# Pair attention with 15 steps a tile: |a| folded into the projections, and VectorE adding the two feature halves of one row block in eight

## What is computed

```
mask = where(adj > 0, 0, -1e22)
q = feat @ W1.T                      # 2048 x 64
k = feat @ W2.T                      # 2048 x 64
e = relu(q[None, :, :] + k[:, None, :])      # for each pair (i, j): 64 features
scores[i, j] = sum_d e[i, j, d] * a[d]
out = softmax(scores + mask) @ feat
```

## Time and profile before

| | |
|---|---|
| median of three runs | 12600.37 us (12598.65 to 12601.54) |
| profiled execution, span | 12601.2 us |
| TensorE busy | 12319.6 us (98%) |
| VectorE busy | 9716.6 us (77%) |
| ScalarE busy | 9590.5 us (76%) |
| mean granted TensorE clock | 0.993 |
| matmuls of the pair stage (L1254) | 7128.4 us busy |

### The profile page before, as it was taken

How to read it: one execution, slowest core, us unless ns; L and a number is a source line. 1 busy time by engine, 2 the same in 40 slices (tenths; PEclk the granted TensorE clock), 3 DMA queues, 4 the chain that set the end, 5 groups by cost and what they waited for, 6 DMA issues and landing times.

```text
span 12601.2 us, 250115 instructions
## 1 busy us (share of the span) xinstructions
PE 12319.6 (98%) x109953; PEld 6079.0 (48%) x109953; DVE 9716.6 (77%) x13670; ACT 9590.5 (76%) x8545; POOL 419.2 (3%) x636
## 2 busy tenths in 40 slices
PE   7999999999999999999999999999999999999999
PEld 3333853338533384333843338433384334843348
DVE  4888848888488885888758887588875888758887
ACT  3888748887488874888749887488874888758886
POOL 1000000000000000000000000000000000000000
PEclk9999999999999999999999999999999999999999
DMA  2000320003200031000310003100031000310003
GB/s 76 20 19 18 103 81 21 18 18 110 78 18 18 18 117 70 18 18 18 126 61 18 18 22 129 54 18 18 23 137 46 18 18 27 139 40 18 21 24 107
DMA packets 205754, 610.39 MB, mean 48 GB/s; under 512 B 45057, under 2 KB 136833, under 8 KB 139137
## 3 DMA queue, kind: packets, MB, share of 16 engines
q1 hardware_dynamic: 183792, 450.72, 10.4%
q0 software_dynamic: 20880, 143.66, 3.1%
HBM read 556.47 MB, written 8.39 MB: 45 GB/s over the span
## 4 chain that ended last, share of the span: by engine, by line
PE 91%; DVE 7%; ACT 1%; issue 1%; SPq 0%; DMA 0%; POOL 0%; DVEq 0%
PE ps L1254 53%; PE ps L1236 10%; PE ps L1338 7%; PE ps L1351 4%; PE ps L1411 4%; PE ps L1267 4%; PE ps L1318 4%; PE ps L1176 2%; PE ps L1397 2%; DVE E L799 1%; DVE E L800 1%; DVE PT L826 1%; PE ps L1219 1%; DVE T L922 1%; DVE E L801 1%
## 5 line engine op out<-in xcount | busy, mean ns | idle before, releaser
L1254 PE MATMUL ps<-E,a_win 128*32 128x512 f32 x65536 | 7128.4, 594 | 31.0 <-ACT E L566 19.6
L1254 PEld LDWEIGHTS ps<-E,a_win 128*32 128x32 f32 x65536 | 2136.4, 110 | 4827.8 <-issue 4683.3
L566 ACT ACTIVATE E<-Q,ka 128x2048 f32<-128x2048 f32 x2048 | 4075.4, 1990 | 0.0
L799 DVE TENSOR_SCALAR E<-Q,kd 128x2048 f32<-128x2048 f32 x2048 | 2630.4, 1284 | 982.4 <-PE ps L1254 957.5
L565 ACT ACTIVATE E<-Q,ka 128x1280 f32<-128x1280 f32 x2048 | 2786.2, 1360 | 783.6 <-PE ps L1254 759.6
L800 DVE TENSOR_SCALAR E<-Q,kd 128x2048 f32<-128x2048 f32 x2048 | 2625.5, 1282 | 0.0
L801 DVE TENSOR_SCALAR E<-Q,kd 128x768 f32<-128x768 f32 x2048 | 1265.6, 618 | 0.0
L922 DVE CUSTOM_DVE_ANT_0 T<-ps,adj_ring 128x2048 f32<-128x2048 f32 x512 | 1172.1, 2289 | 88.7 <-PE ps L1318 85.9
L599 ACT ACTIVATE T<-T,nmin 128x2048 f32<-128x2048 f32 x512 | 1028.1, 2008 | 217.2 <-DVE nmin L922 217.1
L1338 PE MATMUL ps<-ident,T 128*128 128x128 f32 x8192 | 1098.5, 276 | 17.1 <-DVE HT L884 12.3
L1338 PEld LDWEIGHTS ps<-ident,T 128*128 128x128 f32 x8192 | 913.1, 141 | 198.7 <-ACT PT L471 71.0
(11 more groups left out here) (131 smaller groups left out, 7578.1 us busy)
## 6 DMA issues: line engine op xcount, KB each, us to landing
adj_ring<-in_adj SPq DMA_DIRECT2D x384, 1024.0 KB, 5.1
adj_res<-in_adj POOLq DMA_DIRECT2D x128, 1024.0 KB, 6.5
qcur<-AGG SPq DMA_DIRECT2D x896, 16.0 KB, 2.8
qcur<-HT SPq DMA_DIRECT2D x896, 16.0 KB, 2.2
HW<-in_x POOLq DMA_DIRECT2D x9, 1024.0 KB, 7.2
X<-in_x SPq DMA_DIRECT2D x128, 64.0 KB, 1.9
out_x<-X SPq DMA_DIRECT2D x8, 1024.0 KB, 17.0
wq_r<-in_L_gnn_Wq SPq DMA_DIRECT2D x4, 64.0 KB, 2.6
```

The lines of the kernel that those rows point to most:

```text
L566: nc.scalar.activation(E[:, s + 3, :], Q2[:, :], ACT.Relu, bias=ka[:, u, 48 + m:49 + m]).then_inc(e_act, 1)
L799: nc.vector.tensor_scalar(E[:, s, :], Q2[:, :], kd[:, u, m:m + 1], 0.0, ALU.add, ALU.max)
L1254: last = mm(ps[QROWS * grp:QROWS * (grp + 1), 4 * u + c, :], win, E[:, s + grp, c * CH:(c + 1) * CH], start=(m == 0), stop=(m == QUADS - 1 ...
```

## The change

**One row is now half the features of four rows i.** Partitions hold 32 features of four rows. A tile's 32 row blocks (8 in each of the four column groups) have a first half (features 0 to 31) and a second half (32 to 63), 64 rows of E as before. `QA` and `QB` hold the queries of either half four times over, `KLO`, `KHI`, `KBN` and `KBP` the keys of all tiles, made once a batch.

**|a| is folded into the projections.** Since |a| relu(q + k) is relu(|a|q + |a|k), the weights are scaled by |a| with signs when the program starts, and `s_win` holds only signs. Keys are held negated (all but `KBP`), and relu(q + k) is written as max(q, -k) (they differ by k, which is the same for all j and drops out of the softmax). A first half is given the sign of its second half's a: where the signs agree it is max(QA, KLO), else min(QA, KHI), so its operation is a maximum and a minimum with two per-partition scalars, one of which has no effect. ScalarE still makes a relu, with `KBP` as bias.

**One block in eight is added up before TensorE.** With like signs in both halves, VectorE can add them: in one block of each column group it makes the first half and then, with one scalar_tensor_tensor, adds max(QB, KBN) to it in place. That block takes one row of E, not two. A column group has 7 x 2 + 1 = 15 rows, a tile 15 steps of 4 (`NS`). `PLAN` says for each step and column group which half or sum it is and whether ScalarE makes it: 26 second halves a tile go to ScalarE, all whole rows; VectorE makes 28 first halves alone, 4 sums and 2 second halves. Every slot of E now comes round after three steps.

**Around it.** Each chunk of queries takes two matmuls, the keys 8 of 256 columns a half; VectorE copies the QB chunks and makes the key tables from PSUM, ScalarE copies QA. Keys of the first half go ahead of the last chunk's queries. `PT1` is now a name for HW, so that x is fetched behind the stage. The tail's places move with the shorter tile: minimum after step 1, exp after 3, transposes after 5, both copies after 7, product after 9, `finish1` after 11. Eight small loads and 15 more small VectorE operations stand at the program's start.

The diff, cut to its core:

```diff
 EQ = 3
-SPLIT = 768
-TURN = QUADS + QUADS // 2
+FUSED = (4, 8, 6, 12)
+NS = 2 * SETS - 1
+SCALAR_TWO = tuple(k for k in range(NS) if k != 1)
+def column_group(g):
+    kinds, m = [], 0
+    while len(kinds) < NS:
+        if len(kinds) == FUSED[g]:
+            kinds.append(("fused", m))
+        else:
+            kinds += [("first", m), ("second", m)] if g < 2 else [("second", m), ("first", m)]
+        m += 1
+    return kinds
+def tile_plan():
+    plan = []
+    for row in zip(*[column_group(g) for g in range(4)]):
+        left = 2 if len(plan) in SCALAR_TWO else 1
+        step = []
+        for kind, m in row:
+            by_act = kind == "second" and left > 0
+            left -= by_act
+            step.append((kind, m, by_act))
+        plan.append(step)
+    return plan
...
+        PT1 = HW
...
             for k in range(LN_EARLY, LN_MID):
                 rstd_step(b, k)
+            pool.wait_ge(x2_rdy, (b + 1) * NT)
+            fetch(b + 1 if more else b)
             fetched_rstd(b + 1)
...
-            def quad(T, m, u, first):
-                nc.scalar.activation(E[:, s + 2, SPLIT:N], Q2[:, SPLIT:N], ACT.Relu, bias=ka[:, u, 32 + m:33 + m])
-                nc.scalar.activation(E[:, s + 3, :], Q2[:, :], ACT.Relu, bias=ka[:, u, 48 + m:49 + m]).then_inc(e_act, 1)
+            def step1(b, t, k):
+                n = t * NS + k
+                if n >= EQ:
+                    act.wait_ge(e_used, b * NT * NS + n - EQ + 1)
+                for g, (kind, m, by_act) in enumerate(PLAN[k]):
+                    if by_act:
+                        col = k_col(t, g, m)
+                        last = nc.scalar.activation(E[:, e_slot(t, k) + g, :], QB[:, :], ACT.Relu, bias=KBP[:, col:col + 1])
+                last.then_inc(e_act, 1)
...
+            def evac_k1(b, half):
+                dve.wait_ge(qk1_ps, b * 10 + (7, 10)[half])
+                nc.vector.tensor_scalar(KBP[:, cols], of_b, -1.0, None, ALU.mult)
+                nc.vector.tensor_copy(KBN[:, cols], of_b)
+                nc.vector.tensor_scalar(KLO[:, cols], of_a, same[:, :], low_off[:, :], ALU.mult, ALU.add)
+                nc.vector.tensor_scalar(KHI[:, cols], of_a, other[:, :], high_off[:, :], ALU.mult, ALU.add).then_inc(k1_sb, 1)
...
+                add = None
+                for g, (kind, m, by_act) in sorted(enumerate(PLAN[k]), key=lambda x: x[1][0] != "fused"):
+                    if by_act:
+                        continue
+                    if kind == "second":
+                        last = nc.vector.tensor_scalar(dst, QB[:, :], KBN[:, col:col + 1], None, ALU.max)
+                    else:
+                        last = nc.vector.tensor_scalar(dst, QA[:, :], KLO[:, col:col + 1], KHI[:, col:col + 1], ALU.max, ALU.min)
+                    if kind == "fused":
+                        last.then_inc(e_first, 1)
+                        add = dst, col
+                if add:
+                    dve.wait_ge(e_first, (b * NT + t) * 4 + at + 1)
+                    last = nc.vector.scalar_tensor_tensor(out=dst, in0=QB[:, :], scalar=KBN[:, col:col + 1], in1=dst,
+                                                          op0=ALU.max, op1=ALU.add)
+                last.then_inc(e_dve, 1)
...
+                evac_qb(b, 0)
                 normalise(b, LN_1, chunk_of(NC - 1), X, H, zn_rdy)
+                evac_qb(b, 1)
+                evac_qb(b, 2)
+                evac_k1(b, 0)
+                evac_qb(b, 3)
...
+            def keys1(b, half):
+                pe.wait_ge(qa_sb, b * NC + half + 1)
+                rows = HT[:, :].rearrange("p (n r) -> p n r", r=GR)
+                for at, w in ((0, wka), (256, wkb)):
+                    for r in range(GR):
+                        last = mm(ps[GP * r:GP * (r + 1), 4 + half, at:at + 256], w[:, :],
+                                  rows[:, half * 256:(half + 1) * 256, r], start=True, stop=True,
+                                  tile_position=(0, GP * r))
+            def queries1(b, c):
+                for bank, w in ((4 + c, wqa), (c, wqb)):
+                    mm(ps[:, bank, :], w[:, :], HT[:, c * CH:(c + 1) * CH], start=True, stop=True).then_inc(qk1_ps, 1)
...
                 for c in range(NC):
-                    for grp in range(4):
-                        last = mm(ps[QROWS * grp:QROWS * (grp + 1), 4 * u + c, :], win,
-                                  E[:, s + grp, c * CH:(c + 1) * CH], start=(m == 0), stop=(m == QUADS - 1),
-                                  tile_position=(0, QROWS * grp))
+                    for g, (kind, m, by_act) in enumerate(PLAN[k]):
+                        win = s_win[:, QROWS - GR - GR * m:2 * QROWS - GR - GR * m]
+                        last = mm(ps[QROWS * g:QROWS * (g + 1), 4 * u + c, :], win,
+                                  E[:, s + g, c * CH:(c + 1) * CH], start=(k == 0), stop=(k == NS - 1),
+                                  tile_position=(0, QROWS * g))
```

## The result

The changed kernel takes 12303.23 us (median of 4 runs, 12302.36 to 12303.74), the kernel before, run beside it, 12600.96 (4 runs, 12598.65 to 12601.7). The ratio is 0.9764, with a 95% interval of 0.9751 to 0.9778: 2.4% faster. The forecast was 12364 us, 61 us too much; that lies within its own range, 13 us above its lower end.

The account below looks back on a forecast made before the run. TensorE was taken to bound the pair stage before, VectorE to set the tile after. 8 x (-33.1 + 2.7) + 6.5 = -236.7 us on 12601.2 gave 12364 us; own range 12,290 to 12,440.

Parts of the forecast that it names:

- The two-pointer first half: VectorE's first half with KLO and KHI at 128x2048: 1.35 us long, 1.265 start to start, a pointer costing 0.063.
- case 1: Pair stage: TensorE still sets the tile if the second pointer costs nothing; some 57.6 us a tile, 12,175 us; chance 0.10.
- VectorE's sum 57.6 and a wait of 1.2: Pair-stage tile: VectorE's work of 57.6 us plus a 1.2 us wait at `finish1` for the value product, 58.8 us.
- The layer-norm tiles: Three of the 15 intervals between tiles hold four layer-norm operations, charged 1.0 us each; average 59.08 us after.
- The average before, 61.17: Pair stage before the change: mean of tiles of 60.87 and 61.47 us, from which the 59.08 after was subtracted.
- the forecast's first tile: First tile of the pair stage, without tail: 60.2 us before, 58.5 after, paced by VectorE, 1.7 less.
- The seam, +2.7 us a batch: Before the pair stage: keys ahead of the last query product +1.0, two query matmuls +1.9, VectorE's earlier copy -0.2.
- The start, +6.5 us: Program start, once: eight more small loads 4.4 us, fifteen tiny VectorE operations and five waits 2.1; range 4 to 10.
- The fetch of x at no cost: Next x's fetch moves on POOL behind the stage: 45 us of cover, no cost; uncovered, up to 10 us a batch.
- Case 2: Pair stage: VectorE sets the tile with more waits than found; at 1 us more a tile, 12,492 us; chance 0.17.
- Case 3: VectorE's first halves: the second pointer takes the double pace away, 2.33 us start to start, 16,730 us; chance 0.07.
- case 4: Pair stage: the tile doesn't shorten, VectorE's waits adding up to TensorE's old pace; about 12,600 us; chance 0.04.

## Why the prediction was right, and where its sizes were off

The mechanism held: the step that goes shortens TensorE's tile, VectorE takes over as the bound, and the tile ends where VectorE's sum and its one wait put it. TensorE's standstill is smaller than forecast, 0.8 us a tile and not 1.4, and stands at one of the four fused steps alone. The last transposes ahead of the stage stand at 250.22 and 11218.79 us in the first and the last batch before, at 251.47 and 10956.41 after: a batch takes 1566.9 us before and 1529.3 after, 37.6 less, where the sum had 33.1 - 2.7 = 30.4. That is 58 us over eight, and the start gives the other 5. The terms one by one:

**The two-pointer first half, 1.265 start to start.** It is 1.257 [the row of 436.60]. The duration of 1.339 stands against 1.35. Over 32 operations that is 0.3 us a tile. The experiment with one pointer gives the second pointer 0.060 us; the rows before gave 0.063 and 0.054, and the price was the right one to argue on, as it decided between this case and case 1. The Trainium skill's table, "VectorE: DVE Perf Modes", section "The perf-mode tier table (the rule you actually need)", has 1227 ns for this shape without a charge for pointers; no form with a pointer agrees with it here (1279 for one, 1339 for two).

**VectorE's sum 57.6 and a wait of 1.2: 58.8 us a tile.** The wait is 1.28, the tile 58.40, so the sum is 57.1: 0.5 less, of which the first halves are 0.3. This is one mis-sized term. The layer-norm tiles go the other way: the forecast gave each of the three 1.0 us more than a plain tile, and it is 1.7 (60.09 against 58.40), with the slot wait of 0.49 among it.

**The average before, 61.17.** I took the mean of two plain tiles. The rows behind them show that three of 14 intervals were longer before as well. TensorE's timeline before, and after:

```profile
338.62 1.97 PE L1176 MATMUL ps<-ident,T 128*128 128x128 f32 x16
...
583.29 1.97 PE L1176 MATMUL ps<-ident,T 128*128 128x128 f32 x16
...
613.86 0.66 PE L1304 MATMUL ps<-ident,AGG 128*128 128x128 f32 x4
...
645.49 1.97 PE L1176 MATMUL ps<-ident,T 128*128 128x128 f32 x16
...
1197.16 1.97 PE L1176 MATMUL ps<-ident,T 128*128 128x128 f32 x16
```

```profile
337.10 1.97 PE L1270 MATMUL ps<-ident,T 128*128 128x128 f32 x16
...
1160.24 1.97 PE L1270 MATMUL ps<-ident,T 128*128 128x128 f32 x16
```

From 583.29 to 645.49 it is 62.20 us: TensorE makes four transposes of normalised features there (L1304), on top of the longer tile's work. I charged the layer-norm work to the tiles after and not to those before. Over the 14 intervals of batch 0, from 338.62 to 1197.16 before and from 337.10 to 1160.24 after, the mean is 61.32 before (forecast 61.17) and 58.80 after (forecast 59.08): 2.53 a tile and not 2.09. The 0.44 are the largest mistake: 6.2 us a batch, 49 in all, a third of it the average before and two thirds the tile after.

**The rest of the stage.** The stage is 980.1 - 941.2 = 38.9 us shorter, and 33.1 were forecast. The 14 intervals give 35.4; its two ends give 3.5, where the forecast's first tile and one more interval make 1.7 + 2.1 = 3.8.

**The seam, +2.7 us a batch (bounds 1 and 5).** In batch 0 the first write of E came 4.3 us behind the start of the last transposes (250.22, key copy at 254.31 and 0.2 long); it comes 5.3 behind them after. That is +1.0, at the lower bound. (Sixteen key matmuls follow the last transposes there, and not eight; the eight of the second half are done at 257.88, while VectorE writes the first rows, and TensorE then waits 2.9 us for its first step.) TensorE and VectorE there, after:

```profile
251.47 0.66 PE L1277 MATMUL ps<-ident,H 128*128 128x128 f32 x4 [1.05 <-ACT H L528]
252.06 1.09 PE L1286 MATMUL ps<-HT,wka 128*32 128x256 f32 x8
...
253.98 1.13 PE L1294 MATMUL ps<-HT,wqa 128*128 128x512 f32 x2
254.94 1.02 PE L1294 MATMUL ps<-HT,wqb 128*128 128x512 f32 x2
```

```profile
256.79 2.60 DVE L881 TENSOR_SCALAR E<-QA,KLO,KHI 128x2048 f32<-128x2048 f32 x2
```

The term that was mis-sized is the 2.08 us that I carried over for the last query product: it takes 1.13, its partner 1.02. The windows show the clock: for before the stretches ahead of batch 1's transposes and from there to the first step, for after the same, and the first 3 us of the stage (columns as in the earlier trace rows):

```profile
1813.03:1818.03 5.00, 1.59 (x3) 0.30 (x3) 2.71 (x13) 1.25 (x3) 2.99 (x4) 0.61 0.00 2
1818.03:1826.26 8.23, 5.10 (x11) 1.54 (x11) 3.65 (x5) 5.28 (x7) 1.30 (x1) 0.50 0.00 0
```

```profile
1776.08:1781.08 5.00, 1.98 (x4) 0.68 (x5) 4.00 (x16) 1.25 (x3) 2.99 (x4) 1.00 0.00 0
1781.08:1790.38 9.30, 6.43 (x41) 2.04 (x41) 6.81 (x10) 5.67 (x6) 1.30 (x1) 1.00 0.00 0
1790.38:1793.38 3.00, 3.00 (x16) 0.95 (x20) 3.00 (x3) 3.00 (x2) 0.00 (x0) 0.51 0.02 5
```

Before, the clock is at its lower level (0.50, 1.2 GHz) throughout this seam of batch 1; after, it is at 1.00 (2.4 GHz) there and falls to the lower level at the stage's first step, where TensorE has waited 2.9 us and VectorE sets the pace anyway. In four batches, the first among them, a low stretch lies ahead of the transposes too (0.66 in the 5 us before 251.47). In batch 1 the seam is only +0.55: the first write of E stands 4.77 behind the transposes before (1822.80) and 5.32 after (1786.40). Taking 0.6 a batch, the term was 2.1 too large, 17 us over eight. The prediction had named the doubt ("that may have changed by then"), but took the slow value; the seams of the other batches would not have settled it, as the query pair takes 2.08 us in all of them before.

**The start, +6.5 us.** SP's queue and POOL, which answer to the earlier trace rows:

```profile
6.38 3.90 SPq L372 DMA_DIRECT2D a<-in_L_gnn_a  x8
```

```profile
36.72 8.44 POOL L498 DMA_DIRECT2D adj_res<-in_adj  x16
```

The eight loads take 3.90 us (4.4 were said), and the adjacency is issued at 36.72, 5.3 later than before. TensorE's first product with it starts at 59.35, and it started at 56.98: +2.4 us, and at the first seam only 1.25 are left (251.47 against 250.22). I let the whole delay of the issue through to the end: 5.2 us too much.

**The fetch of x at no cost.** It is issued at 1213.62, behind the stage, and VectorE first reads HW at 1268.02, 54 us later and without a wait, as in the earlier trace rows:

```profile
1213.62 1.23 POOL L484 DMA_DIRECT2D HW<-in_x  x1
```

```profile
1268.02 0.29 DVE L1155 BATCH_NORM_STATS2 xstats<-HW 128x6 f32<-128x128 f32 x1
```

Together: stage 8 x 5.8 = 46, seam 17, start 5, which makes 68; 63 were to be found. The 5 us between, 0.7 a batch, lie behind the pair stage or in the seams of other batches, and I didn't follow them.

**The rivals.** Case 1 (TensorE sets the tile, 12,175) didn't happen, but it names the bound that stands next: three versions reach it, at 12,170 to 12,174. That its number fits so well is in part luck. It took 57.6 us as the average tile, and over the 14 intervals of batch 0 it is 57.89 with one pointer and 57.76 with the sum at 10; against that it carried the 22 us too much of seam and start. Case 2 (more waits) is wrong: within a plain tile VectorE waits for another engine at `finish1` alone. The remark behind it, that a wait reaches the other engine through the ring, showed in the experiments: to remove the wait of 1.28 us brought 0.15 or 0.5 and not 1.28. Case 3 would have needed 1.32 a first half, and case 4 is what the layout without the sum does.

## What to carry over

Where two engines' sums per tile are within two per cent, look at each engine's sum and its waits before you ask which is "the bound": a wait is free on the engine with time to spare, on the other its removal gives back only the part that doesn't come back at a slot of the ring, and here moving one row of 1.2 us away, together with the sum that TensorE waited behind, brought 133 us where removing the wait brought 14 or 50. An engine with room in its sum can still be late in a stretch: count its rows over the few steps that the ring can hold, not over the tile. When you compare averages, take them over the same kinds of tiles on both sides.

## What the runs showed of the hardware that I had not expected

- A pointer scalar has a price of its own on VectorE: a tensor_scalar of 128x2048 in fp32 takes 1.220 us with none (L896 after), 1.280 with one (L879), 1.339 with two (L881), and 1.279 again when the second is a constant. Over 4096 first halves that is 246 us of VectorE's time, of which 129 reached the end.
- Where TensorE's clock is at its lower level varies between batches of one kernel that issue the same work. With the keys behind the queries, batch 0 runs the query pair in 2.08 us and batch 2 in 1.12, both behind transposes and 0.69 us of idleness; in the changed kernel the seam is at full pace in all eight batches (granted clock 0.99 or 1.00), and a low stretch lies in the stage's first step in all of them (0.50 to 0.58 in its first 3 us) and ahead of the seam in four. What it costs depends on whether TensorE is waited for where it falls; I could not say from these traces what places it.
